# A macaron transformer block in fp32: the negated row maxima turned on VectorE in 32 by 32 squares instead of on TensorE

## What is computed

```python
x = x + 0.5 * ffn(layernorm(x))
x = x + attn(layernorm(x))       # 16 heads of 32, 2 batches
x = x + 0.5 * ffn(layernorm(x))

scores = einsum('bhqd,bhkd->bhqk', q, k) * SCALE
probs  = softmax(scores)
attn   = einsum('bhqk,bhkd->bhqd', probs, v)
```

## Time and profile before

| | |
|---|---|
| median of 3 runs | 2859.27 us (2858.29 to 2860.98) |
| the profiled execution | 2860.46 us, span 2858.5 us |
| PE busy | 2843.2 us (99%) |
| DVE busy | 2064.1 us (72%) |
| ACT busy | 1607.2 us (56%) |
| POOL busy | 1368.6 us (48%), most of it in the attention |
| granted TensorE clock | 0.999 of full speed |

### The profile page before, as it was taken

One profiled execution on the slowest core, in us unless ns is written; L12 is line 12 of the kernel. 1 busy time (PEld: TensorE's weight loads), 2 busy tenths in 40 slices (PEclk: granted clock), 3 DMA queues, 4 the chain that ended last, 5 costly groups with the idle time before them and its releaser, 6 DMA issues.

```text
span 2858.5 us, 38081 instructions
## 1 busy us (share of the span) xinstructions
PE 2843.2 (99%) x14334; PEld 1950.8 (68%) x14334; DVE 2064.1 (72%) x3084; ACT 1607.2 (56%) x2851; POOL 1368.6 (48%) x486
## 2 busy tenths in 40 slices
PE   9999999999999999999999999999999999999999
PEld 7888888787755555555555555555555568888887
DVE  5655556778888888888888888888888456665553
ACT  6444434333276767676776767676767654333333
POOL 0000000000089998999898989898989720000000
PEclk9999999999999999999999999999999999999999
DMA  5111112555489998999999999999999972222200
GB/s 192 32 57 30 30 30 76 196 202 181 149 179 196 194 211 192 197 211 195 210 197 192 215 192 199 208 198 207 199 192 202 213 206 60 59 60 59 74 15 30
DMA packets 134983, 424.29 MB, mean 148 GB/s; under 512 B 23824, under 2 KB 41488, under 8 KB 98832
## 3 DMA queue, kind: packets, MB, share of 16 engines
q0 software_dynamic: 31824, 231.75, 39.4%
q1 hardware_dynamic: 102976, 190.11, 23.2%
HBM read 121.91 MB, written 67.63 MB: 66 GB/s over the span
## 4 chain that ended last, share of the span: by engine, by line
PE 96%; DVE 2%; ACT 1%; issue 0%; POOL 0%; DMA 0%; SPq 0%; DVEq 0%; ACTq 0%
PE bank L1142 18%; PE bank L1138 17%; PE bank L1172 16%; PE bank L636 16%; PE bank L642 16%; PE bank L808 7%; PE bank L497 3%; PE bank L1199 1%; PE bank L276 0%; ACT att_p L1122 0%; DMA qkv_raw<-upT 0%; DVE qkv_o_lo L772 0%; DVE norm_cent L122 0%; DVE norm_inv L186 0%; PE bank L1161 0%
## 5 line engine op out<-in xcount | busy, mean ns | idle before, releaser
L1053 DVE TENSOR_REDUCE att_row_max<-bank 128x1 f32<-128x512 f32 x2048 | 1249.1, 681 | 208.3 <-PE bank L1142 208.2
L1002 POOL TENSOR_TENSOR att_acc<-att_acc,att_p 128x2048 f32<-128x2048 f32 x216 | 1072.9, 4967 | 18.9 <-ACT att_p L1122 12.2
L1122 ACT ACTIVATE att_p<-bank 128x512 f32<-128x512 f32 x1792 | 919.2, 617 | 286.2 <-PE bank L1138 281.3
L1142 PE MATMUL bank<-att_k,att_q 96*128 96x512 f32 x2048 | 833.9, 409 | 1.3 <-DVE att_row_max L1053 1.3
L1138 PE MATMUL bank<-att_q,att_k 98*128 98x512 f32 x2048 | 810.2, 399 | 3.4 <-ACT att_p L1122 3.4
L1142 PEld LDWEIGHTS bank<-att_k,att_q 96*128 96x128 f32 x2048 | 387.2, 189 | 273.5 <-DVE att_row_max L1053 122.2
L1138 PEld LDWEIGHTS bank<-att_q,att_k 98*128 98x128 f32 x2048 | 386.7, 189 | 113.3 <-ACT att_p L1122 15.6
L618 ACT ACTIVATE ffn_hid<-bank,up_s 128x512 f32<-128x512 f32 x256 | 176.2, 688 | 507.4 <-PE bank L636 493.5
L569 DVE TENSOR_TENSOR ffn_hid_lo<-ffn_hid,ffn_hid_hi 128x512 fp32r<-128x512 f32 x256 | 175.2, 691 | 364.2 <-ACT ffn_hid_hi L621 363.9
L1172 PE MATMUL bank<-att_p,att_v 128*32 128x512 f32 x3584 | 433.6, 600 | 0.0
L636 PE MATMUL bank<-hi,ffn_up_w 128*128 128x512 f32 x1024 | 399.0, 390 | 2.8 <-DVE lo L221 1.5
(11 more groups left out here) (123 smaller groups left out, 2405.1 us busy)
## 6 DMA issues: line engine op xcount, KB each, us to landing
att_dma_acc<-att_p POOLq DMA_DIRECT2D x161, 1024.0 KB, 10.5
att_dma_acc<-att_dma_acc POOLq DMA_DIRECT2D x30, 1024.0 KB, 12.1
att_dma_acc<-att_acc POOLq DMA_DIRECT2D x30, 1024.0 KB, 6.9
att_q<-q_hi SPq DMA_DIRECT2D x64, 256.0 KB, 4.1
att_k<-k_hi SPq DMA_DIRECT2D x64, 256.0 KB, 6.4
x<-x_after_ffn SPq DMA_DIRECT2D x14, 1024.0 KB, 7.2
x_after_ffn<-x_out SPq DMA_DIRECT2D x8, 1024.0 KB, 9.5
q_hi<-qkv_o_hi SPq DMA_DIRECT2D x32, 256.0 KB, 2.0
```

What stands on the lines that cost most here:

```text
L1002: self.nc.gpsimd.tensor_tensor(self.acc[H % 2][:], a[:], self.tile(H, kt)[:], ALU.add).then_inc(self.summed, 1)
L1053: self.nc.vector.tensor_reduce(self.row_max[odd][:, qt, q:q + 1], m[:], axis=AX.X, op=ALU.max).then_inc(self.m_read, 1)
L1122: self.nc.scalar.activation(into[:, q * CH:(q + 1) * CH], self.score_bank(H, kt, q)[:], ACT.Exp, scale=SCALE).then_inc(self.exp_done, 1)
L1142: self.nc.tensor.matmul(m[:], self.q_st[T % NB][0:KQ, qt * P:(qt + 1) * P], self.k_st[T % NB][0:KQ, q * CH:(q + 1) * CH], start=True, stop ...
```

## The change

The turn moves to DVE. `neg_max` is now 128 x 32 with 16 columns in use (set to zero once), and four transposes of 32 by 32 take its four squares side by side into the rows of `neg_t`, 32 x 128, in SBUF; its first 16 rows are the turned maxima. The upper and the lower part are made from there, so both operands of the subtraction and the source of the cast lie in SBUF and no longer in PSUM. `rows_out` follows `negate` at once. PE's product, its waits and its slot in the ring of banks are gone, and the row sums keep the one slot behind block 44 (`SUMS_SLOT = SUMS_AT`). For the last two heads' row sums, which share a bank, PE waits for ACT's copy. Of the diff, the moved addresses and renamed semaphores are left out:

```diff
-SUMS_AFTER = TURN_AFTER = 4
-SUMS_AT = TURN_AT = GROUP_ENDS[SUMS_AFTER]
-SLOTS = UNITS + 2
+SUMS_AFTER = 4
+SUMS_AT = GROUP_ENDS[SUMS_AFTER]
+SLOTS = UNITS + 1
...
-NEG = 3
+TURN = 32
+NEG = 3 + P // TURN
...
-    return p + (p >= SUMS_AT) + (p >= TURN_AT)
-TURN_SLOT, SUMS_SLOT = TURN_AT, SUMS_AT + 1
+    return p + (p >= SUMS_AT)
+SUMS_SLOT = SUMS_AT
...
     def negate(self, dve, H):
         dve.wait_ge(self.m_read, UNITS * (H + 1))
         if H > 0:
-            dve.wait_ge(self.neg_pe, H)
-        self.nc.vector.tensor_reduce(self.neg_max[:], self.row_max[H % 2][:], axis=AX.X, op=ALU.max, negate=True).then_inc(self.neg_dve, 1)
-
-    def rows_out(self, dve, H, t_ps):
-        dve.wait_ge(self.neg_pe, H + 1)
+            dve.wait_ge(self.neg_dve, NEG * H)
+        else:
+            self.nc.vector.memset(self.neg_max[:], 0.0).then_inc(self.neg_set, 1)
+            dve.wait_ge(self.neg_set, 1)
+        self.nc.vector.tensor_reduce(self.neg_max[:, 0:KT], self.row_max[H % 2][:], axis=AX.X, op=ALU.max, negate=True).then_inc(self.neg_dve, 1)
+
+    def rows_out(self, dve, H):
+
+        dve.wait_ge(self.neg_dve, NEG * H + 1)
+        for i in range(P // TURN):
+            part = slice(i * TURN, (i + 1) * TURN)
+            self.nc.vector.transpose(self.neg_t[:, part], self.neg_max[part, :]).then_inc(self.neg_dve, 1)
+        dve.wait_ge(self.neg_dve, NEG * (H + 1) - 2)
         if H > 0:
             dve.wait_ge(self.neg_loaded, 32 * H)
-        self.nc.vector.tensor_copy(self.neg_hi[:], t_ps[0:KT, 0:P]).then_inc(self.neg_dve, 1)
-        dve.wait_ge(self.neg_dve, NEG * H + 2)
-        self.nc.vector.tensor_tensor(self.neg_lo[:], t_ps[0:KT, 0:P], f32(self.neg_hi[:]), ALU.subtract).then_inc(self.neg_dve, 1)
+        self.nc.vector.tensor_copy(self.neg_hi[:], self.neg_t[0:KT, :]).then_inc(self.neg_dve, 1)
+        dve.wait_ge(self.neg_dve, NEG * (H + 1) - 1)
+        self.nc.vector.tensor_tensor(self.neg_lo[:], self.neg_t[0:KT, :], f32(self.neg_hi[:]), ALU.subtract).then_inc(self.neg_dve, 1)
...
             if kt == KT - LEAD and q == 0 and H + 1 < NH:
                 self.negate(dve, H + 1)
-            if p == TURN_AT - 1 and H + 1 < NH:
-                self.rows_out(dve, H + 1, self.turn_bank(H))
+                self.rows_out(dve, H + 1)
...
-        if u == TURN_AFTER and H + 1 < NH:
-            self.bank_free(pe, H, TURN_SLOT)
-            self.transpose_max(pe, H + 1, self.turn_bank(H))
         if u == sums_after(H) and H > 0:
             self.bank_free(pe, H, SUMS_SLOT)
+            if H == NH - 1:
+                pe.wait_ge(self.head_out.sums_copied, H - 1)
             self.sums(pe, H - 1)
```

More of the change, by code:

```diff
@@ L928, in __init__ @@
         self.row_max = [c.sb(f"att_row_max{i}", HEAD_AT + 4 + 0.25 * i, [P, KT, QC]) for i in range(2)]
-        self.neg_max = c.sb("att_neg_max", HEAD_AT + 4.5, [P, KT])
-        self.neg_hi, self.neg_lo = c.sb("att_neg_hi", HEAD_AT + 5, [KT, P], F32R), c.sb("att_neg_lo", HEAD_AT + 5.5, [KT, P], F32R)
+        self.neg_max, self.neg_t = c.sb("att_neg_max", HEAD_AT + 4.5, [P, TURN]), c.sb("att_neg_t", HEAD_AT + 4.8750, [TURN, P])
+        self.neg_hi, self.neg_lo = c.sb("att_neg_hi", HEAD_AT + 5.375, [KT, P], F32R), c.sb("att_neg_lo", HEAD_AT + 5.875, [KT, P], F32R)
         self.m_ps, self.s_ps, self.o_ps = c.bank[0:4], c.bank[4:7], c.bank[7]
@@ L935, in __init__ @@
         self.m_ready, self.m_read = c.sem("att_m_ready"), c.sem("att_m_read")
-        self.neg_dve, self.neg_pe, self.neg_loaded = c.sem("att_neg_dve"), c.sem("att_neg_pe"), c.sem("att_neg_loaded")
+        self.neg_set, self.neg_dve, self.neg_loaded = c.sem("att_neg_set"), c.sem("att_neg_dve"), c.sem("att_neg_loaded")
         self.s_ready, self.exp_done, self.p_used = c.sem("att_s_ready"), c.sem("att_exp_done"), c.sem("att_p_used")
@@ L949, in sums_bank @@
         return self.m_ps[3] if H >= NH - 2 else self.m_ps[m_bank(H + 1, SUMS_SLOT)]
-    def turn_bank(self, H):
-        return self.m_ps[m_bank(H, TURN_SLOT)]
     def load(self, sp, X, pieces=range(6)):
@@ L977, in max_rows @@
         for r, rows in enumerate((self.neg_hi, self.neg_lo)):
-            sp.wait_ge(self.neg_dve, NEG * H + 2 + r)
+            sp.wait_ge(self.neg_dve, NEG * (H + 1) - 1 + r)
             sp.dma_start(f32(self.q_st[H % NB][KQ + r:KQ + r + 1, :].rearrange("o (t p) -> o t p", p=P)),
@@ L1154, in first_maxima @@
             pe.wait_ge(self.m_read, n - 1)
-        if n == UNITS:
-            pe.wait_ge(self.neg_dve, NEG)
         self.maxima(self.first_bank(n), T, n % UNITS // QC, n % QC)
-    def transpose_max(self, pe, H, t_ps):
-        pe.wait_ge(self.neg_dve, NEG * H + 1)
-        self.nc.tensor.transpose(t_ps[0:KT, 0:P], self.neg_max[:], self.ident[:]).then_inc(self.neg_pe, 1)
     def out_tile(self, pe, H, kt):
@@ L1208, in bank_free @@
             pe.wait_ge(self.head_out.sums_copied, H)
-        elif old == TURN_SLOT:
-            pe.wait_ge(self.neg_dve, NEG * (H + 2))
         elif old < 0:
@@ L1487, in _ @@
                             att.negate(dve, 0)
-                        if (n, t) == FIRST_TURN:
-                            att.rows_out(dve, 0, att.m_ps[2])
+                            att.rows_out(dve, 0)
                 for H in range(NH):
@@ L1604, in _ @@
                             att.first_maxima(pe, first + b)
-                        if (n, t) == FIRST_TURN:
-                            att.transpose_max(pe, 0, att.m_ps[2])
                 pe.wait_ge(qkv.qk_read, 8 * NCH)
@@ L1618, in beside @@
                                 pe.wait_ge(att.m_read, UNITS * NH)
-                                pe.wait_ge(att.neg_dve, NEG * NH)
                                 pe.wait_ge(wo_done, DT + 1)
```

## The result

The kernel with the change takes **2874.3 us** (median of 6 runs, 2869.95 to 2877.01), the kernel before 2860.12 in 6 runs beside it: ratio 1.0047, interval 1.0038 to 1.0057. It is slower, by 14.2 us between the medians, and 1.3 us above the end of the predicted range. The profiled execution took 2872.1 with a span of 2870.1, 11.6 more than the span before. The granted clock was 0.996 over the span, where it had been 0.999. Single executions of 5590 us and more, which occurred with the kernel before and in experiments 1 and 8, are in no median or ratio here.

A forecast was written before the change was run, and what follows sets the result against it. PE was taken to bound the kernel (96% of the work that ended last). The median 2859.27 plus 4.2, the middle between +5.6 (POOL following PE's delays) and +2.9 (POOL on its own clock), gave 2863.5 us, range 2850 to 2873.

The forecast's parts named there:

- head 30's turn: Last turn in the heads' loop: no maxima behind it, transfers at most 2 us later and covered; -0.3 us.
- E: Time from the negation's start to the end of POOL's addition; a turn costs E - 2.33 us where positive.
- head 0: Turn of the first head: POOL's addition ends 4.81 us after the negation, DVE returns late; +3.2 us.
- PE's saving: In each of 31 turns PE loses its identity product and some shape-change cost: 0.30 us a turn, 9.2 in all.
- The squares: Four 32x32 transposes on DVE at each turn: 0.21 us each, 0.84 in all, bounds 0.4 and 2.8.
- Rival (B): At the turns the squares are held up by POOL as well: about +28 us, 2887, or some 2868; chance 0.06.
- The cast held until POOL's addition ends: At the turns the cast waits for POOL's running addition; both copies done about 0.40 us after it ends; chance 0.70.
- Rival (A): At the turns the copies are not held up by POOL: all 9.2 us stay, 2850.1; chance 0.18.
- The 28 turns: Turns of heads 2 to 29: 11.4 us lost against 8.4 gained, +3.0; +0.3 with POOL on its own clock.
- the middle I took: Whole sum: +4.2 us, between +5.6 with POOL following PE's delays fully and +2.9 with POOL on its own clock.
- Rival (D): The change doesn't do what it says, such as PE still waiting through the ring of banks; given no chance of its own.
- Rival (C): In the heads POOL's DMA chains set the pace, freed PE time becomes waits for tiles: about half the gain, 2855; chance 0.06.

The follow-up runs named there:

- Experiment 1: The changed kernel, with POOL made to wait in head 30, after line 468's scaling, until DVE has written the turned maxima: 2865.34 us, ratio 1.0022 to the kernel before.
- experiment 8: The changed kernel with the upper part made by a reduction and POOL's additions of the probabilities replaced by fills: 2850.7 us, ratio 0.9971.
- experiment 2: The changed kernel with the four squares written into a PSUM bank, cast and subtraction reading there, and the ring's turn slot back: 2849.3 us, ratio 0.9966.
- experiment 3: The changed kernel with the upper part made by a reduction over one element in place of the cast: 2864.6 us, ratio 1.0017.
- experiment 4: The kernel before, PE's product kept, with one more DVE copy to SBUF and both parts made from there: 2880.75 us, ratio 1.0068.
- experiment 7: The changed kernel with POOL's first addition of each head replaced by a fill, the others over 512 of 2048 columns: 2858.63 us, ratio 1.0005.

## Why the prediction was wrong, and where it was right

**The step that failed** is the one on head 30's turn: "head 30's turn has no maxima behind it", with SP's transfers "at most 2 us later than now", "13 us" ahead of the next head, "covered". It listed E for 30 turns and left the last out, and took for granted that a hold ends with the addition that is running. There POOL has four instructions in a row, the cast was held 17.58 us, the transfers came 17 us later and not 2, and PE waited 6.04 us for them and then worked at half clock, together +9.1 where -0.3 stood. Experiment 1 takes the row apart and the 9.1 is gone. The rows that should have warned are in POOL's timeline of the kernel before, as closely packed at that turn (its negation is at 2233.20) as after it:

```profile
2231.55 5.48 POOL L468 TENSOR_TENSOR op_raw<-op_raw,op_inv_first 128x2048 f32<-128x2048 f32 x1
2236.07 5.43 POOL L1002 TENSOR_TENSOR att_acc<-att_acc,att_p 128x2048 f32<-128x2048 f32 x1
2241.15 5.76 POOL L472 TENSOR_TENSOR lo<-op_raw,hi 128x2048 fp32r<-128x2048 f32 x1
2245.64 5.80 POOL L1002 TENSOR_TENSOR att_acc<-att_acc,att_p 128x2048 f32<-128x2048 f32 x1
```

POOL was read at the turns of heads 0 and 29 and not at head 30's. The sentence "if that cover went, the next head's start would slip" named the effect and gave it no chance.

**A term that was mis-sized:** head 0, +4.45 for +3.2. DVE was late by what had been worked out, 5.07 after the negation where 5.21 stood (4.81 + 0.40). Behind it came the lower clock, which the sum didn't have: 1.7 us by the windows, of which 1.3 shows in the period.

**Right, step by step:**
- PE's saving: 0.33 a turn for 0.30.
- The squares: 0.90 for four, 0.84 taken, with one SBUF operand and never held. Rival (B) is out.
- The cast held until POOL's addition ends: it ends at E + 0.09 (0.1 taken) and DVE, where that is late, is back at E + 0.33 (0.40 taken), at 29 of the 31 turns in the heads' loop; POOL was idle at head 1's, and head 30's is the exception. Rival (A), not held, is out, and experiments 2, 3 and 4 show that it is the operands' place: with PSUM no hold, with SBUF a hold whichever engine turned the maxima. The Trainium skill (SBUF — State Buffer, "Who interferes with whom") has a cast in a two-port mode share a port pair with GpSimd, and a subtraction with both inputs in SBUF share it with GpSimd's reads; whoever issues first has the pair "for the whole instruction". The cast's median of 1.29 and, without it, the subtraction's of 1.21 agree. The 17.58 us over four instructions is longer than that sentence allows.
- The 28 turns: 0.0 net where +3.0 stood for a POOL that follows PE and +0.3 for one on its own clock. After a long stall E is shorter at the next turn (4.45 at head 2's, 2.03 at head 3's; 4.13, 2.75 and 2.20 at heads 9 to 11), so POOL keeps its own clock, and the middle I took, +4.2 in all, was 1.3 too high for that part.
- Rival (D) is out with the product's row: the change does what it says. Rival (C), POOL's DMA chains: PE's waits don't end on them after the change. In experiment 2, where the holds are gone, POOL makes up 1% and DMAs 2% of the chain that ended last, against 0% each in the kernel before, so it may be what would come next.

Put together with what was then known: +2.9 (POOL on its own clock), +1.3 for head 0's clock, +9.4 for head 30's turn gives 13.6, and the medians are 14.2 apart. The sign was forecast with the mechanism, the range missed by a turn that wasn't looked at. How much that turn cost was in part chance: with a hold almost as long, experiment 3 lost only 0.8 us there.

## What to carry to other kernels

A small tile that DVE casts or subtracts beside a busy POOL belongs in PSUM, even when DVE makes it itself: here that moved the same change from 14.2 us slower to 10.7 us faster. When a hold by another engine is priced, list that engine's queue at every place the instruction stands, the odd last one above all, and look at whether its instructions leave a gap between them, for the long holds here lasted to the first gap and not to the end of one instruction. And a stall of PE can cost more than its length: those of 2.45 and 6.04 us did, one of 1.03 us (experiment 3) did not.

## What was not expected of the hardware

- A held DVE instruction was not let in where the records of two of POOL's arithmetic instructions overlap: 17.58 us over four instructions, 5.80 over two. It was let in at gaps of 0.16 us and 0.48 us between them. One reading of before doesn't fit, the 1.99 us of the earlier trace rows: that subtraction was over at 2313.32, while the comparison's record on POOL runs from 2308.80 to 2314.49. No run explains it.
- A cast that began 0.43 us before the addition's record, during POOL's DMA issue, was held for 5.34 us (experiment 4), and a subtraction that began 0.38 us before one for 2.12 us (experiment 7).
- PE idle for 2.45 us and for 6.04 us was followed by a granted clock of 0.50, the 1.2 GHz level, which cost another 1.3 to 1.7 and 2.8 us. The kernel before has the same once: in head 30 PE waits 2.73 us for ACT, up to 2239.51, and the window from 2240 to 2244 has 0.50. With PE kept at work through the last wait, and with a wait of 1.03 us there, the clock stayed at 1.00.
- A transfer of the same 8 KB (`att_neg_lo`, one to a turn) landed 3.4 to 7.9 us after its issue at head 30's turn, from run to run.
- A transpose of 32x32 fp32 on DVE takes 199 ns from SBUF to SBUF and 215 ns into PSUM.
